# Roots between fewer gathers, scales by register, whole-width weight steps: one edit to a gated-experts kernel

## The reference

```
h  = layernorm(x)                                   # over the 512 columns
e  = min(token_id // 6250, 3)                       # one of 4 experts for each token
a  = h @ ctx[e].T                                   # Wg = Wu = Wd = ctx
x1 = x + tanh(g_xattn) * ((silu(a) * a) @ ctx[e].T)
h2 = layernorm(x1)
out = x1 + tanh(g_ffn) * fp8_linear(h2, weight)     # both quantised to e4m3, one scale each
```

## Time and profile before

| | |
|---|---|
| median of 3 runs | 205.53 us (205.48 to 206.47) |
| the profiled execution | 204.08 us, of which the span from the first to the last instruction is 202.2 us |
| TensorE (PE) busy | 147.7 us, 73% |
| VectorE (DVE) busy | 154.5 us, 76% |
| ScalarE (ACT) busy | 116.7 us, 58% |
| GpSimd (POOL) busy | 86.5 us, 43% |
| mean granted TensorE clock | 0.947 |

### The profile page before, as it was taken

How to read it: one execution, slowest core, us unless ns; L and a number is a source line. 1 busy time by engine, 2 the same in 40 slices (tenths; PEclk the granted TensorE clock), 3 DMA queues, 4 the chain that set the end, 5 groups by cost and what they waited for, 6 DMA issues and landing times.

```text
span 202.2 us, 3155 instructions
## 1 busy us (share of the span) xinstructions
PE 147.7 (73%) x759; PEld 73.7 (36%) x764; DVE 154.5 (76%) x348; ACT 116.7 (58%) x178; POOL 86.5 (43%) x120
## 2 busy tenths in 40 slices
PE   0232949798999999999989999999951285566700
PEld 0101425243555455555544454455420133233200
DVE  2886799879746999987988876556687899998720
ACT  2455596887455755688956562433222987666510
POOL 7167888230334323444467854211111014556670
PEclk9999999999999999999999999999996559999975
DMA  2837998200000000000000000000000002132341
GB/s 49 333 96 199 355 406 269 64 2 0 3 0 0 2 3 0 0 3 0 2 0 0 0 0 0 5 0 0 2 0 0 3 0 83 72 156 104 157 194 66
DMA packets 5646, 13.28 MB, mean 66 GB/s; under 512 B 1024, under 2 KB 1536, under 8 KB 5632
## 3 DMA queue, kind: packets, MB, share of 16 engines
q0 software_dynamic: 2560, 8.39, 11.4%
q1 hardware_dynamic: 2784, 4.73, 6.7%
q10 hardware_dynamic: 288, 0.00, 0.1%
HBM read 8.92 MB, written 4.19 MB: 65 GB/s over the span
## 4 chain that ended last, share of the span: by engine, by line
PE 36%; DVE 29%; ACT 12%; issue 11%; POOL 8%; DMA 1%; DVEq 1%; POOLq 0%
PE four_ps L437 9%; PE four_ps L429 9%; PE four_ps L442 9%; DVE w_hi L1007 3%; PE four_ps L469 3%; DVE hT_hi L1015 3%; POOL z L353 3%; POOL x L322 3%; PE four_ps L543 2%; DVE x L1019 2%; DVE w_lo L792 2%; ACT sg L592 2%; ACT y L671 2%; ACT w L583 2%; DVE bn L800 2%
## 5 line engine op out<-in xcount | busy, mean ns | idle before, releaser
L345 POOL DMA_INDIRECT out<-x,token_of x16 | 19.3, 1208 | 25.4 <-DVE x L1019 23.0
L353 POOL TENSOR_TENSOR z<-az,sg 128x512 f32<-128x512 f32 x15 | 19.0, 1267 | 25.6 <-ACT az L594 17.2
L340 POOL TENSOR_TENSOR rstd<-var,minus_half 128x1 f32<-128x1 f32 x16 | 8.8, 549 | 47.7 <-DVE var L856 47.7
L601 ACT ACTIVATE zT_hi<-four_ps 128x512 f16<-128x512 f32 x19 | 11.3, 595 | 21.5 <-PE four_ps L469 21.5
L592 ACT ACTIVATE sg<-four_ps,job_inv_a 128x512 f32<-128x512 f32 x19 | 13.0, 685 | 17.3 <-PE four_ps L442 15.9
L429 PE MATMUL four_ps<-w_hi,hT_hi 128*128 x76 | 21.4, 393 | 1.4 <-ACT w_hi L570 1.2
L842 DVE SCALAR_TENSOR_TENSOR x<-four_ps,job_mul,x 128x512 f32 x19 | 14.2, 749 | 9.8 <-PE four_ps L442 9.5
L322 POOL DMA_INDIRECT x<-in_x,token_of x16 | 17.4, 1087 | 7.0 <-issue 4.2
L429 PE MATMUL four_ps<-w_hi,zT_hi 128*128 x76 | 19.5, 379 | 0.8 <-ACT zT_hi L601 0.8
L437 PE MATMUL four_ps<-w_lo,zT_hi 128*128 x76 | 19.5, 379 | 0.0
L442 PE MATMUL four_ps<-w_hi,zT_lo 128*128 x76 | 19.5, 379 | 0.0
(11 more groups left out here) (147 smaller groups left out, 301.6 us busy)
## 6 DMA issues: line engine op xcount, KB each, us to landing
w<-in_ctx_t SPq DMA_DIRECT2D x4, 1024.0 KB, 9.5
wf<-in_wf_t SPq DMA_DIRECT2D x1, 512.0 KB, 16.4
x<-in_x,token_of POOLq DMA_INDIRECT x16, 5.9
out<-x,token_of POOLq DMA_INDIRECT x16, 2.7
g_s<-in_g_x ACTq DMA_DIRECT2D x1, 0.5 KB, 2.8
ids_s<-in_ids SPq DMA_DIRECT2D x1, 8.0 KB, 2.6
g_s<-in_g_f ACTq DMA_DIRECT2D x1, 0.5 KB, 6.4
```

The source lines that it names most:

```text
L345: pool.indirect_dma_start(out, bass.IndirectOffsetOnAxis(ap=token_of[:, i:i + 1], axis=0), block_of(x1, i), None, bounds_check=T - 1).then ...
L353: pool.tensor_tensor(z[:, :], az[:, :], sg[:, :], ALU.mult).then_inc(z_done, 1)
```

## The change

- GpSimd's roots rstd_first(0), (1), (2) stand behind gathers 2, 4 and 7 instead of 4, 7 and 11.
- The tables job_is, job_of, job_inv_a and job_z_mul are gone. silu, az and z read the scale column of w_bits at an address that a register holds (scale_of); the register is loaded from job_expert_i by a value_load, in silu on ScalarE for each of 19 jobs and in z_of on VectorE for four. job_mul stays; each job's column is made by a new small VectorE instruction, factor(j), with a value_load of its own, between add_y(j - 1) and zT_low(j), and add_y(j) waits for it.
- For experts 2 and 3 the squares, w_hi and w_lo are one instruction over 2048 columns each. squares_whole(2) and (3) stand behind the first norm in jobs 0 and 1; w_low_whole stands behind shift_first(j + 2).
- ScalarE waits for jobs_ready once, before the squares of expert 1.

```diff
...
@@ -229,6 +225,10 @@
 
         def w_scale(e, n):
             return w_bits[:, e, n:n + 1].bitcast(F32)
+
+        def scale_of(expert, n):
+
+            return w_bits[:, bass.ds(expert, 1), n].bitcast(F32)
 
         def chunk(t, i, k):
 
@@ -373,7 +373,7 @@
             pool.tensor_tensor(pick[:, :, :], hit[:, :, :], token_no[:, :].unsqueeze(2).to_broadcast([P, C, TILES]),
                                ALU.mult).then_inc(pick_done, 1)
             pool.wait_ge(tokens_ready, 1)
-            after_gather = {4: 0, 7: 1, 11: 2}
+            after_gather = {2: 0, 4: 1, 7: 2}
             for i in range(TILES):
                 gather(i)
                 if i in after_gather:
@@ -557,6 +557,17 @@
                 act.wait_ge(hT_done, i + 1)
                 act.activation(block_of(hT_hi, i), hT_ps[:, :], ACT.Copy).then_inc(hT_hi_done, 1)
 
+            def w_all(t, e):
+                return t[:, e * K * D:(e + 1) * K * D]
+
+            def squares_whole(e):
+                act.wait_ge(w_loaded[e], 16)
+                act.activation(w_all(w_lo, e).bitcast(BF16), w_all(w32, e), ACT.Square).then_inc(squares_done, K)
+
+            def w_high_whole(e):
+                act.wait_ge(w_scales, e + 1)
+                act.activation(w_all(w_hi, e), w_all(w32, e), ACT.Copy, scale=w_scale(e, S_W)).then_inc(w_hi_done, K)
+
             def squares(e, chunks=range(K)):
 
                 act.wait_ge(w_loaded[e], 16)
@@ -584,14 +595,15 @@
                     .then_inc(h2_done, 1)
 
             def silu(j):
+                expert = act.value_load(job_expert_i[0:1, j:j + 1], min_val=0, max_val=E - 1)
                 act.wait_ge(a_done, j + 1)
-                if isinstance(j, int) and j < E:
-                    act.wait_ge(job_scales, 2 * (j + 1))
-                if not isinstance(j, int) or j > 0:
+                if j < E:
+                    act.wait_ge(w_scales, j + 1)
+                if j > 0:
                     act.wait_ge(z_done, j)
-                act.activation(sg[:, :], a_ps[:, :], ACT.Silu, scale=job_inv_a[:, bass.ds(j, 1)]).then_inc(silu_done, 1)
+                act.activation(sg[:, :], a_ps[:, :], ACT.Silu, scale=scale_of(expert, INV_A)).then_inc(silu_done, 1)
                 if z_on_pool(j):
-                    act.activation(az[:, :], a_ps[:, :], ACT.Copy, scale=job_z_mul[:, bass.ds(j, 1)])\
+                    act.activation(az[:, :], a_ps[:, :], ACT.Copy, scale=scale_of(expert, Z_MUL))\
                         .then_inc(az_done, 1)
 
             def zT_high(j):
@@ -606,20 +618,16 @@
                     silu(j)
                 if not fixed or j + 1 < TILES:
                     hT_high(j + 1)
-                if fixed and j == 0:
-                    squares(2, range(2))
                 if fixed and 1 <= j and j + 1 < E:
-                    w_high(j + 1)
+                    w_high_whole(j + 1)
                 if not fixed or j > E:
                     norm_second(j - E - 1)
                 if not fixed or j < JOBS:
                     zT_high(j)
                 if not fixed or j + 2 < TILES:
                     norm_first(j + 2)
-                if fixed and j == 0:
-                    squares(2, range(2, K))
-                if fixed and j == 1:
-                    squares(3)
+                if j < 2:
+                    squares_whole(j + 2)
                 if fixed and WF_SCALED <= j < WF_SCALED + K:
                     wf_scaling(j - WF_SCALED)
 
@@ -641,6 +649,7 @@
             w_high(0)
             squares(1, range(1))
             norm_first(0)
+            act.wait_ge(jobs_ready, 1)
             squares(1, range(1, K))
             hT_high(0)
             norm_first(1)
@@ -763,29 +772,6 @@
             dve.tensor_copy(job_expert_i[:, :], job_e[0:1, :]).then_inc(jobs_ready, 1)
             dve.tensor_tensor(job_tile_i[:, :], iota_job[0:1, :], job_e[0:1, :], ALU.subtract).then_inc(jobs_ready, 1)
             w_scaling(0)
-            for e in range(E):
-                ins = dve.tensor_scalar(job_is[:, e, :], job_e[:, :], float(e), None, ALU.is_equal)
-            routed(ins)
-            def add_expert(table, chosen, e, n):
-
-                if e == 0:
-                    return dve.tensor_scalar(table[:, :], chosen[:, 0, :], w_scale(0, n), None, ALU.mult)
-                return dve.scalar_tensor_tensor(out=table[:, e:], in0=chosen[:, e, e:], scalar=w_scale(e, n),
-                                                in1=table[:, e:], op0=ALU.mult, op1=ALU.add)
-
-            def product_tables(e):
-                if e > 0:
-                    dve.wait_ge(job_scales, 2 * e)
-                add_expert(job_inv_a, job_is, e, INV_A).then_inc(job_scales, 1)
-                add_expert(job_z_mul, job_is, e, Z_MUL).then_inc(job_scales, 1)
-
-            def result_table(e):
-                if e > 0:
-                    dve.wait_ge(job_factors, e)
-                add_expert(job_mul, job_of, e, INV_Y).then_inc(job_factors, 1)
-
-            product_tables(0)
-
             def w_low(e, chunks=range(K)):
                 for k in chunks:
                     dve.wait_ge(w_hi_done, K * e + k + 1)
@@ -793,6 +779,18 @@
                                              in1=w_block(w_hi, e, k), op0=ALU.mult, op1=ALU.subtract)\
                         .then_inc(w_lo_done, 1)
 
+            def w_low_whole(e):
+                dve.wait_ge(w_hi_done, K * (e + 1))
+                cols = slice(e * K * D, (e + 1) * K * D)
+                dve.scalar_tensor_tensor(out=w_lo[:, cols], in0=w32[:, cols], scalar=w_scale(e, S_W),
+                                         in1=w_hi[:, cols], op0=ALU.mult, op1=ALU.subtract).then_inc(w_lo_done, K)
+
+            def factor(j):
+
+                expert = dve.value_load(job_expert_i[0:1, j:j + 1], min_val=0, max_val=E - 1)
+                dve.tensor_tensor(job_mul[:, j:j + 1], mask[:, j:j + 1], scale_of(expert, INV_Y), ALU.mult)\
+                    .then_inc(job_factor, 1)
+
             def stats_first(i):
 
                 if isinstance(i, int):
@@ -823,10 +821,11 @@
 
             def z_of(j):
 
+                expert = dve.value_load(job_expert_i[0:1, j:j + 1], min_val=0, max_val=E - 1)
                 dve.wait_ge(silu_done, j + 1)
                 if j > 0:
                     dve.wait_ge(zT_done, j)
-                dve.scalar_tensor_tensor(out=z[:, :], in0=a_ps[:, :], scalar=job_z_mul[:, j:j + 1], in1=sg[:, :],
+                dve.scalar_tensor_tensor(out=z[:, :], in0=a_ps[:, :], scalar=scale_of(expert, Z_MUL), in1=sg[:, :],
                                          op0=ALU.mult, op1=ALU.mult).then_inc(z_done, 1)
 
             def zT_low(j):
@@ -836,6 +835,7 @@
             def add_y(j):
 
                 tile = dve.value_load(job_tile_i[0:1, bass.ds(j, 1)], min_val=0, max_val=TILES - 1)
+                dve.wait_ge(job_factor, j + 1)
                 dve.wait_ge(y_done, j + 1)
                 if not isinstance(j, int) or j > 0:
                     dve.wait_ge(x1_done, j)
@@ -903,10 +903,6 @@
                 routed(dve.tensor_tensor(mask[:, :], slot_e[:, :], job_e[:, :], ALU.is_equal))
                 dve.wait_ge(tanh_done, 1)
                 routed(dve.tensor_scalar(mask[:, :], mask[:, :], tg[:, 0:1], None, ALU.mult))
-                routed(dve.tensor_tensor(job_of[:, :, :], job_is[:, :, :],
-                                         mask[:, :].unsqueeze(1).to_broadcast([P, E, JOBS]), ALU.mult))
-                result_table(0)
-                result_table(1)
 
             def job(j):
 
@@ -925,7 +921,6 @@
                     z_of(j)
                 if fixed and 1 <= j and j + 1 < E:
                     w_scaling(j + 1)
-                    w_low(j + 1, [0])
                 if not fixed or j > E + 1:
                     max_second(j - E - 2)
                 if not fixed or j + 1 < TILES:
@@ -936,11 +931,11 @@
                     masks()
                 if fixed and 1 <= j and j + 1 < E:
                     shift_first(j + 2)
-                    w_low(j + 1, range(1, K))
-                    product_tables(j + 1)
-                    result_table(j + 1)
-                if not fixed or 1 <= j <= JOBS:
+                    w_low_whole(j + 1)
+                if 1 <= j <= JOBS:
                     add_y(j - 1)
+                if j < JOBS:
+                    factor(j)
                 if not fixed or E - 1 <= j < TILES - 2:
                     shift_first(j + 2)
                 if not fixed or E <= j < TILES + E:
@@ -962,7 +957,6 @@
             hT_low(0)
             shift_first(1)
             w_scaling(1)
-            product_tables(1)
             stats_first(2)
             w_low(1, [0])
             var_first(2)
```

More of the change, by code:

```diff
@@ L114, in gated_experts_kernel @@
         w_bits = sb("w_bits", [P, E, 4], I32)
-        job_is = sb("job_is", [P, E, JOBS], F32)
         table_loaded = sb("table_loaded", [P, 1], F32)
-        job_of = sb("job_of", [P, E, JOBS], F32)
-        job_inv_a = sb("job_inv_a", [P, JOBS], F32)
```

(3 more changed lines are left out.)

## The result

The changed kernel is **slower**: 208.89 us against 206.13, ratio 1.0134 [1.0103, 1.0166] over 16 runs of each. The profiled execution took 209.18 us, span 207.2, mean granted clock 0.927.

A forecast was written before the change was run, and what follows sets the result against it. The prediction took the start of down(2), held by GpSimd's queue up to z(1), as what bounds the kernel. Terms -1.45 + 0.80 + 0.1 + 0.2 = -0.35 us gave 205.2 us, range 203.8 to 206.8.

The forecast's parts named there:

- rival B: TensorE's clock falls in the longer idle ahead of z(1), slowing up(2): +0.3 to +2.1 us, middle 206.4; chance 0.2.
- a granted clock of 0.5 near 36 us: Sign named in advance that would make the prediction wrong: TensorE's clock at 0.5 near that time.
- z(1) moves later by 0.80 us: On GpSimd, the last gather and z(1) come 0.80 us later, bounds 0.03 and 0.9.
- The wait of root 0: On GpSimd behind gather 2, root 0 waits for its variance from 15.37 to 16.17: 0.80 us, new.
- three slow gathers: Gathers of 1.21 to 1.31 us on GpSimd, 0.77 us over the usual in sum; forecast to stay.
- From the end of z(1) to down(2), -1.45: Steps between z(1) and down(2) take 12.6 us instead of 14.07: 1.45 us less, bounds 1.2 and 1.65.
- The hand-offs: Between z(1) and down(2): three uncovered hand-offs between engines of about 0.06 us each, and 0.07 to the start of w_hi.
- Whole width by itself wins little: Whole-width w_hi takes 1.99 us for 2.56, but TensorE and VectorE can no longer start on the first chunk.
- Loads and factor: In each job: register loads and addresses cost 0.1 us (bounds 0 and 0.5), factor 0.2 (bounds 0 and 1.1).
- About five jobs: Number of jobs in which the later silu was to cost 0 to 0.05 us each.
- Rival C: Register loads not hidden on ScalarE in about twelve jobs: +5.3 us, 210.5; chance 0.05.
- Rival A: Slow gathers do not come back, z(1) moves by 0.03 only: -1.1 us, 204.4; chance 0.25.

The follow-up runs named there:

- roots_later: The changed kernel with its three roots behind gathers 3, 5 and 8 instead of 2, 4 and 7; 208.10 us, ratio 1.0100 to the kernel before.
- after_filled: The changed kernel with 14 unread products on TensorE in the idle stretch ahead of the transposes of z(1); 206.88 us, ratio 1.0039 to the kernel before.
- before_again: The kernel before, unchanged, profiled a second time; that execution took 206.68 us.
- whole_only: The kernel before with only the whole-width squares, w_hi and w_lo of experts 2 and 3; 205.64 us, ratio 1.0009.
- roots_filled: The kernel before with roots behind gathers 2, 4 and 7, plus 14 unread TensorE products ahead of the transposes of z(1); 205.77 us, ratio 0.9982.
- roots_only: The kernel before with only the three roots moved, behind gathers 2, 4 and 7; 206.01 us, ratio 0.9997.
- registers_only: The kernel before with only the tables removed, scales read by register, and factor; roots and chunks as before; 206.10 us, ratio 1.0020.

## Why the prediction was wrong

**The clock, a term that the sum does not have.** The sum adds up three things: z(1) later, the steps behind it shorter, loads and factor dearer. Each went the way that was forecast and each came out worse. The largest loss, 2.12 of 3.73 us, is none of them: TensorE's clock, which the sum put at nothing and left to rival B. One of the prediction's own signs of being wrong, a granted clock of 0.5 near 36 us, is what came.

**"z(1) moves later by 0.80 us": mis-sized, 1.65.** The wait of root 0 was right (0.88). The three slow gathers of the earlier trace rows gave way to one of 1.53 us, 0.76 - 0.51 = 0.25 us less; dense transfers, my reason for keeping all three, do not slow a gather by themselves: after, of the five gathers that start between 20 and 28 us, where the DMA engines are busy throughout, four take 1.01 to 1.06. What was missing is the roots themselves: they take 1.01 + 0.57 + 1.11 = 2.69 us where the three before took about 0.58 + 0.60 + 0.58 = 1.76. Together 0.88 + 0.93 - 0.25 = 1.56, and 0.09 in hand-offs. Roots 0 and 2 now fall on chunks of w_lo on VectorE, at 16.05 and 24.18: root 0 ends at 17.23, 0.44 us behind the end of the one (16.79), root 2 at 26.00, 0.42 behind the end of the other (25.58). The Trainium skill (SBUF — State Buffer, "Who interferes with whom") states that a VectorE instruction with two SBUF inputs contends with a GpSimd instruction that reads SBUF, and that such contention is an exclusive lock. The rows agree, and so does roots_later, where root 0 starts as a w_lo ends and takes 0.58, while root 2 falls on a pair of them and takes 1.12. I had applied the rule to the new whole-width w_lo and wrote that no root falls into it; I had not asked it of the old chunks at the roots' new places. No run moved w_lo away, so the block is read from rows and was not tried by itself.

**Rival B decided.** It was the right mechanism with too small a chance (0.2). The idle of 3.65 us (forecast: 3.1 or more) cost 2.15 us by after_filled, at the top of its +0.3 to +2.1, of which I had taken the middle. Of the sixteen executions of the change eleven have spans of 206.8 to 207.4 us, longer than any of after_filled (206.1 at most), so by their spans the clock fell in most of them. The earlier trace rows showed one idle stretch on each side, and I weighted them by the length of the idle alone. roots_later and before_again show that the length does not decide by itself: the clock fell behind 2.35 and 3.29 us and stayed behind 2.76. The Trainium skill (TensorE: Matmul & The Clock Gate, "HAM oscillation — how this bites in real kernels") states that waits between bursts of matmuls can bring the clock down; the trace after agrees (3.65 us idle, then 0.50).

**"From the end of z(1) to down(2), -1.45": -0.89 with the clock held.** after_filled gives 50.93 - 37.75 = 13.18 us for 14.07; the forecast was 12.6, outside its bounds. The large steps were right to 0.02 us each (root, w_hi, w_lo, silu, az, z). The hand-offs were too small. In the rows after they are 0.15 (up(2) to silu, 44.04 to 44.19), 0.13 (az to z, 45.46 to 45.59), 0.10 (w_bits to w_hi, 46.87 to 46.97), 0.11 (w_hi to w_lo, 48.97 to 49.08) and 0.13 (w_lo to the product, 51.43 to 51.56), 0.62 in all, where I had 0.07 and three of 0.06, 0.25. And the last third with the transposes took 53.08 - 51.56 = 1.52 us, not 0.87 + 0.43: in these rows a product that is waited for overlaps nothing in front of it. The two, 0.37 + 0.22, come to the 0.58 that was missing; one more hand-off, 0.13 ahead of the third of up(2) in after_filled (40.73 to 40.86), is about made up by overlaps at the root and between silu and az.

**"Whole width by itself wins little."** It loses 0.64 us where w_hi of expert 2 stands behind z(1) (whole_only). The gain of this term comes from the roots: 1.76 us with chunks (roots_filled), 0.89 with whole width and registers (after_filled).

**Loads and factor: 0.3 forecast, 0.84 measured.** The mechanism was right (silu 0.1 us late behind up, factor exposed in some jobs), but both were too small, 0.1 for some 0.5 and 0.2 for 0.35. "About five jobs" was short: of the fifteen intervals from job 3 on, eight grew by 0.05 us or more. Rival C did not happen: the load itself stays hidden, and only the address shows. Rival A did not: of the slow gathers one stayed, and the roots took the place of the others.

**Sum.** 1.65 - 0.89 + 2.12 + 0.84 = 3.72 of the 3.73 us in the jobs, by the profiles, where the forecast had -0.35; 2.12 is the clock, 15.30 - 13.18. Part of it (at most 0.23 us in the jobs) the kernel before also loses in its usual executions. That roots_only was level although its profile shows down(2) 1.63 us late fits the spans given under before_again: its usual executions lack the extra low stretches behind the last job that the kernel before usually has. Why they lack them stays open.

## What to carry to other kernels

An operation moved forward in an in-order queue moves everything behind it backward by what it waits or takes longer at its new place; look for what stands at the end of that queue and who meets there, and move that first (the early z(1), 2.1% with the new root places, did what the early roots alone did not). Price each GpSimd instruction at its new place by what VectorE does at that moment, not by its duration at the old one. Where a change lengthens TensorE's idle time ahead of a stage that TensorE bounds, count the slow products behind it as the likely case, and profile the old kernel twice before comparing single profiles.

## What the runs showed of the hardware

The same code ran at differently granted clocks from execution to execution: up(0) in before_again ended 0.5 us earlier than in the first profile of the same kernel, and the clock fell in the idle stretch behind it, which was longer by as much; registers_only shows the same two (up(0) ends at 24.98, 3.29 us idle, clock down). One extra stretch at 0.50 behind the last job goes with about 1.1 us, two with about 2.3. A root of 128 elements on GpSimd, 0.57 us by itself, took 1.0 to 1.1 us beside VectorE's w_lo, and in the change ended 0.42 to 0.44 us behind the end of it.
